# Moving most of an attention stage beside the first quarter of a selective scan, in a one-core fusion kernel on Trainium2

## The chip, the cores and the metric

The kernel runs on one NeuronCore of one Trainium2 chip. A core has a matrix engine (PE, TensorE; its weight loads are listed as PEld), a vector engine (DVE), a scalar engine (ACT), GpSimd (POOL), and SP, which here only issues transfers. The engines run their own instruction lists and meet at semaphores. The metric is the device time of the kernel in microseconds (us); lower is better.

## What is computed

Sixteen images of 3 x 128 x 128 become 64 patch tokens each (width 192), pass a 12-head attention, are joined with 32 text tokens each, and go through a selective scan and a quantized feed-forward layer, both added to the residual.

```python
t = conv(x, conv_w, stride 16) + conv_b              # 16 x 64 tokens x 192
q, k, v = (t @ w.T + b for w, b in ...)              # 12 heads of 16
out = softmax(q k^T / 4) v ; h = out @ wo.T + bo
h = concat([h, txt], axis=1)                         # 16 x 96 x 192
# selective scan on layernorm(h): D_IN = 384, N = 16 states
xi, res = split(layernorm(h) @ W_in); xc = silu(causal_conv4(xi))
delta = softplus(x_dbl[:48] @ W_dt + b_dt)           # x_dbl = xc @ W_x, also gives B and C
y = scan(xc, delta, A, B, C) + xc * D ; h = h + (y * silu(res)) @ W_out
h = h + ffn(layernorm(h))                            # two linear layers with quantized activations and weights
```

## The kernel before

**Quarters, blocks and steps.** The 16 images are four quarters of 4 images (4 x 96 = 384 tokens). The scan of a quarter is 24 steps: the 384 channels are 3 blocks of 128, and each block has 8 steps of two states each. Step g of the 96 is: ACT `decay` (L972, two exponentials of 128x384 into PSUM), POOL `times_b` (L457, the scan's input), DVE `scan` (L1278), ACT `guards` (L981, two), DVE `guard_states` (L1287, or L1284 on steps 1, 4 and 6 of a block), then the product with C, on POOL (`times_c`, L463) in five steps of eight and on DVE (L1293) in steps 1, 4 and 6, and PE `sum_y` (L787), which adds the product up in PSUM. ACT works one step ahead with `decay`, POOL two ahead with `times_b`.

**Everything else of the scan's stage and of the feed-forward layer lies beside the steps.** A table `AT` of step numbers says at which step each piece of work of each quarter is put. Every engine goes through the steps in order and issues there what is due, in the order of its own `beside`, `amid` or `after`; no engine looks ahead. Work that uses a PSUM bank is a job: `begin` on PE waits until the reader of the bank's last job has left it. Banks 0 to 4 belong to the scan, 5 to 7 to the jobs.

**The attention precedes the scan.** PE makes the tokens of all 16 images (the helper at L585, 24 products of 128x512, two instructions each), then queries, keys and values. A pair of images is one round: POOL `block_keys` (L416) multiplies the keys of a pair by a head mask into a block-diagonal `kbd`; PE `scores`; DVE takes the maxima and subtracts them (`softmax_in`, L1190 and L1193); ACT exponentials (L1089); PE `turn_prob` (L650), ACT copy (L1084); PE `values`; DVE `softmax_out` (L1200, L1203); PE `turn_out` (L673), ACT copy (L1099); PE `project`; DVE `add_bo` (L1209) writes the result into `h`. The eight pairs are pipelined in a loop written by hand. Quarter 0's mixer (norm, `xi` and `z` products, the causal convolution L1233, `silu_u` L1249, the products with W_x and W_dt, the softplus L952 to L962 and L1255 to L1270) is placed by hand into the last rounds, and quarter 1's norm and `xi` into the steps -6 to 2.

**Transfers.** SP issues all loads at the start in one list, then `rows(q)`: eight transfers of 768 KB which spread B and C of the quarter, stored by ACT (L945) to DRAM, over the 128 lanes of `bc`. Before the scan `bc` holds the images' patches, the attention's queries and keys, and the convolution's weights, so quarter 0's `rows` waits for the last `scores`.

```python
for g in range(STEPS):            # DVE
    scan(g)
    amid(g)
    guard_states(g)
    after(g)
    if on_vector(g):
        times_c(g)
```

## Time and profile before

| what | value |
|---|---|
| median of 3 runs (lowest, highest) | 589.78 us (589.7, 590.13) |
| the profiled execution: its own time | 589.52 us |
| its span, first to last instruction | 587.7 us |
| busy: PE, DVE, ACT, POOL | 404.6, 451.9, 359.1, 411.5 us |
| mean granted TensorE clock | 0.818 of full |
| moved by DMA | 34.35 MB |

A busy time is the union over the instructions of an engine. The granted clock is 1.0 at 2.4 GHz and 0.5 at 1.2 GHz. The profiled execution is 0.3 us from the median of the runs. The rows themselves stand in a section below.

### The profile page before, as it was taken

Reading aid. Unit: us, or ns where it says so; the run is one execution under the profiler, and the core shown is the slowest. Engines: PE = TensorE matmul, PEld = TensorE weight load, DVE = VectorE, ACT = ScalarE, POOL = GpSimd, SP = SyncE. Lnnn points to the kernel's source line nnn. Section 1 sums busy time; section 2 is a strip of 40 time slices with the busy share of each in tenths; the row PEclk is TensorE's granted clock in tenths of the full one; section 3 lists DMA queues with packets and bytes.
Section 4 is the critical chain, followed back from the end, with each engine's and each line's share of the span. In section 5 each row is a group of like instructions: output and inputs, shape, how many; then the busy total and the mean of one; then the engine's idle time right before and its main releaser. Section 6 shows DMA issues by size and latency. Waiting matters only on the chain.

```text
span 587.7 us, 5261 instructions
## 1 busy us (share of the span) xinstructions
PE 404.6 (69%) x1498; PEld 217.9 (37%) x1498; DVE 451.9 (77%) x531; ACT 359.1 (61%) x642; POOL 411.5 (70%) x332
## 2 busy tenths in 40 slices
PE   5998997852697493876665649676755956665553
PEld 2336754431333251543332316333322532332423
DVE  1234644349999999898899898999999799998341
ACT  1135342486689674668775756997657677962353
POOL 2035510094789985879997788799879999988442
PEclk9999998968777685785877988978767797987865
DMA  8900000280000044100004330000154100000000
GB/s 313 196 1 1 2 2 0 86 347 0 1 6 0 26 179 169 58 0 1 0 0 158 124 148 4 20 1 1 44 173 160 54 18 3 1 0 1 20 2 20
DMA packets 10269, 34.35 MB, mean 58 GB/s; under 512 B 2064, under 2 KB 4960, under 8 KB 10016
## 3 DMA queue, kind: packets, MB, share of 16 engines
q1 hardware_dynamic: 9840, 33.23, 16.6%
q10 hardware_dynamic: 400, 0.79, 0.4%
q8 instruction: 12, 0.20, 0.1%
q14 instruction: 17, 0.14, 0.1%
HBM read 32.64 MB, written 1.38 MB: 58 GB/s over the span
## 4 chain that ended last, share of the span: by engine, by line
POOL 36%; DVE 19%; issue 14%; ACT 5%; PE 4%; DVEq 0%; POOLq 0%; ACTq 0%
POOL big L457 15%; POOL big L463 11%; DVE PS L1278 8%; PE PS L585 3%; DVE big L1287 2%; DVE big L1293 2%; ACT PS L972 2%; ACT big L981 2%; POOL big L500 2%; POOL big L481 1%; DVE big L1233 1%; POOL big L475 1%; POOL big L435 1%; POOL big L439 1%; POOL big L490 1%
## 5 line engine op out<-in xcount | busy, mean ns | idle before, releaser
L787 PE MATMUL PS<-big,eighth 128*128 128x384 f32 x384 | 192.1, 640 | 115.5 <-POOL big L463 100.2
L457 POOL TENSOR_TENSOR big<-big,bc 128x768 f32<-128x768 f32 x96 | 179.8, 1882 | 0.0
L1278 DVE TENSOR_TENSOR_SCAN PS<-PS,big 128x768 f32<-128x768 f32 x96 | 168.3, 1753 | 6.4 <-ACT PS L972 4.6
L787 PEld LDWEIGHTS PS<-big,eighth 128*128 128x128 f32 x384 | 87.4, 242 | 201.5 <-POOL big L463 128.6
L972 ACT ACTIVATE PS<-big,Aneg 128x384 f32<-128x384 f32 x192 | 103.8, 573 | 92.7 <-DVE big L1293 56.5
L463 POOL TENSOR_TENSOR big<-big,bc 128x768 f32<-128x768 f32 x60 | 108.7, 1812 | 52.8 <-DVE big L1287 52.5
L981 ACT ACTIVATE big<-big,guard,Ahalf 128x380 f32<-128x380 f32 x192 | 122.2, 690 | 0.0
L1287 DVE SCALAR_TENSOR_TENSOR big<-big,PS 128x768 f32<-128x768 f32 x60 | 56.9, 949 | 5.6 <-DVE PS L1278 0.9
L416 POOL TENSOR_TENSOR big<-bc,cst_sb 96x1536 f32<-96x1536 f32 x8 | 22.0, 2754 | 44.4 <-ACT bc L879 33.3
L585 PE MATMUL PS<-big,w_in_sb 96*128 96x384 f32 x96 | 41.3, 568 | 5.0 <-DVE big L1233 4.4
L585 PE MATMUL PS<-big 128*64 128x34 f32 (+3 forms) x416 | 43.1, 281 | 0.0
L1284 DVE SCALAR_TENSOR_TENSOR PS<-big,PS 128x768 f32<-128x768 f32 x36 | 34.7, 963 | 3.8
L585 PEld LDWEIGHTS PS<-big 96*64 96x64 f32 (+2 forms) x416 | 30.1, 144 | 15.5 <-issue 14.0
L426 POOL TENSOR_SCALAR rstd<-bmv 96x4 f32<-96x4 f32 x4 | 2.8, 688 | 45.5 <-DVE bmv L1223 45.3
L1293 DVE TENSOR_TENSOR big<-PS,bc 128x768 f32<-128x768 f32 x36 | 34.1, 947 | 0.2
L585 PEld LDWEIGHTS PS<-big,w_in_sb 96*128 96x128 f32 x96 | 21.6, 231 | 22.2 <-issue 13.7
L585 PE MATMUL PS<-f_in_q,big 96*96 96x512 bf16 x64 | 23.7, 492 | 6.9 <-DVE big L1323 5.4
L585 PE MATMUL PS<-bc 128*96 128x512 f32 x48 | 23.3, 649 | 6.7 <-DMA bc<-in_cw_dram 6.7
L784 PE MATMUL PS<-big,diagD 128*128 128x384 f32 x24 | 16.5, 784 | 14.4 <-DVE big L1299 14.4
L500 POOL TENSOR_TENSOR big<-big,g_out_bc 96x512 f32<-96x512 f32 x16 | 20.1, 1262 | 7.8 <-ACT big L1017 7.8
L1190 DVE TENSOR_REDUCE big<-PS 128x12 f32<-128x768 f32 x8 | 7.6, 952 | 21.5 <-PE PS L585 21.5
L1023 ACT ACTIVATE big<-big,magic 96x512 f32<-96x512 f32 x16 | 11.9, 802 | 19.9 <-POOL big L519 19.0
(139 smaller groups left out, 560.6 us busy)
## 6 DMA issues: line engine op xcount, KB each, us to landing
bc<-bc_rows SPq DMA_DIRECT2D x32, 768.0 KB, 4.4
bc<-in_x_cols_dram SPq DMA_DIRECT2D x3, 512.0 KB, 6.7
bc<-in_x_cols_dram SPq DMA_DIRECT2D x1, 1536.0 KB, 10.0
out_dram<-h SPq DMA_DIRECT2D x4, 288.0 KB, 2.7
big<-in_f_in_dram SPq DMA_DIRECT2D x1, 768.0 KB, 12.4
bc<-in_cw_dram ACTq DMA_DIRECT2D x1, 576.0 KB, 5.9
w_in_sb<-in_w_in_dram SPq DMA_DIRECT2D x1, 576.0 KB, 16.9
big<-in_f_out_dram SPq DMA_DIRECT2D x1, 384.0 KB, 14.6
```

The lines of the kernel that those rows point to most:

```text
L416: P.tensor_tensor(kbd[:, p % 2], kT[:, hf, :, c:c + 128].unsqueeze(2).broadcast_to([F, 2, HPT, 128]), headmask.unsqueeze(1).unsqueeze(3).b ...
L457: P.tensor_tensor(pair(vR[:, g % VRING]), part(du, q, m).unsqueeze(1).broadcast_to([128, PAIR, QT]), rows_of(g, 0), ALU.mult).then_inc(sem ...
L463: P.tensor_tensor(v, v, rows_of(g, 1), ALU.mult).then_inc(sem("c_pool"), 1)
L500: P.tensor_tensor(yf[:, b], yf[:, b], g_out_bc[:, :], ALU.mult).then_inc(sem("yg_ready"), 1)
L585: return pe.matmul(o_, l_, r_, start=start, stop=stop)
L787: ins = pe.matmul(y_sum, eighth[:, :], vR[:, g % VRING, QT * e:QT * (e + 1)], start=False, stop=True, skip_group_check=True)
L972: ins = A.activation(state_of(g, e), part(delta, q, m), ACT.Exp, scale=Aneg[:, PAIR * j + e, m:m + 1])
L981: ins = A.activation(gR[:, g % GRING, QT * e:QT * (e + 1)].rearrange("p (b l) -> p b l", b=QB)[:, :, 0:L - 1], lt[:, :, 1:L], ACT.Tanh, bi ...
L1278: V.tensor_tensor_scan(h_, h_, vR[:, g % VRING], 0.0, ALU.mult, ALU.add).then_inc(sem("scan_done"), 1)
L1284: V.scalar_tensor_tensor(states(g), gR[:, g % GRING], 1.0, states(g), ALU.add, ALU.mult).then_inc(sem("guarded_here"), 1)
L1287: V.scalar_tensor_tensor(vR[:, g % VRING], gR[:, g % GRING], 1.0, states(g), ALU.add, ALU.mult).then_inc(sem("guarded"), 1)
L1293: V.tensor_tensor(pair(vR[:, g % VRING]), pair(states(g)), rows_of(g, 1), ALU.mult).then_inc(sem("c_vector"), 1)
```

## The change

Names of the new kernel are its own; its line numbers differ from those of the kernel before.

- **Patches by quarters.** The product that makes tokens is done quarter by quarter (`patch`, 256 columns instead of 512), and so are queries, keys and values (`project_tokens`, `values_of_tokens`). The weights `cw` come in three transfers instead of one.
- **Only quarter 0's attention (pairs 0 and 1) is ahead of the scan.** The scores of pair 2 and the patches of quarters 2 and 3 are placed at steps -13 to -10, while quarter 0's softplus runs; the patches' copies out of PSUM (`patch_out`) stand in ACT's list at steps 0 and 1. Pairs 3 to 7, and the rest of pair 2, are placed in steps 0 to 22. So are queries, keys and values of quarters 2 and 3, quarter 0's `z`, and quarter 1's norm, `turn` and `xi`, which preceded or opened the scan before.
- **Attention work becomes jobs** in the table `AT`, with the banks 5 to 7 from step -12 on; before that step all eight banks serve. The softmax goes by halves of six heads (128x384 instead of 128x768).
- **Key blocks by DMA.** POOL's `block_keys` is gone. `kbd` is set to zero once, and SP copies the keys of each head into its diagonal block: six transfers a quarter of 16 lanes.
- **SP's list.** Text tokens are loaded by quarters, each after the quarter's value product; `w_in` and what follows stand behind quarter 0's key blocks. `rows(0)` waits, from its sixth transfer on, for the last patch product of quarter 3, and key blocks of quarters 2 and 3 follow behind it.
- **Quarter 0's mixer** runs by blocks of 128 channels (`silu_u` and its tanh too); its norm is applied by DVE (`normed`) instead of ACT; the quantization of the feed-forward weights is split in two pieces that stand in DVE's list at steps -21 and -16.
- From step 24 on the table is unchanged.

```diff
-FIRST_MIXER = dict(stats=-6, root=-6, xn=-5, turn=-5, turned=-4, xi0=-3, xi1=-2, xi2=-2, tap0=0, tap1=0, tap2=1,
...
-FIRST_STEP, LAST_STEP = -6, STEPS + 32
...
+for p, steps in enumerate((
+        dict(sc0=-29, sc1=-29, si0=-29, si1=-28, ex0=-29, ex1=-28, tp0=-27, tp1=-26, pt0=-27, pt1=-26, vo=-25, so=-25,
...
+        dict(sc0=-13, sc1=-13, si0=-13, si1=-13, ex0=-11, ex1=-11, tp0=-10, tp1=-10, pt0=0, pt1=0, vo=1, so=1,
+             to=2, at=2, pj=3, ab=3),
...
+for p, first in ((4, 5), (5, 7), (6, 13), (7, 16)):
+    AT.update({(name, p): first + r for name, r in dict(
+        sc0=0, sc1=1, si0=0, si1=1, ex0=1, ex1=2, tp0=2, tp1=3, pt0=2, pt1=3, vo=4, so=4, to=5, at=5, pj=6, ab=6).items()})
+AT.update({("ws", 0): -26, ("wmean", 0): -24, ("f_in", 0): -21, ("f_out", 0): -16})
+FIRST_STEP, LAST_STEP, WIDE_BEFORE = -32, STEPS + 32, -12
...
     for i, key in enumerate(JOBS):
-        open_ = range(6, 8) if i < FRONT_JOBS else range(5, 8) if i < WIDE_FROM else range(8)
-        left = AT.get((LAST_READ["%s%d" % (key[0], key[2])], key[1]), FIRST_STEP - FRONT_JOBS + i)
+        open_ = range(8) if JOB_STEP[key] < WIDE_BEFORE or i >= WIDE_FROM else range(5, 8)
...
+            def key_blocks(q):
+                job_left(sp, "k", q, 0)
+                if q == 0:
+                    sp.wait_ge(sem("kbd_set"), 1)
+                else:
+                    job_here(sp, "sc", 2 * q - 1, 1)
+                for j in range(HPT):
+                    lanes = slice(HD * j, HD * (j + 1))
+                    sp.dma_start(kbd[lanes, :, j, :], kT[lanes, :, :]).then_inc(sem("ld_kbd"), 16)
...
+            def text(q):
+                job_here(sp, "v", q, 0)
+                load("txt", h[NP:L, QB * q:QB * (q + 1), :], txt[QB * q:QB * (q + 1)].rearrange("b l d -> l b d"))
...
-            load("ffn", f_out_raw, f_out.rearrange("p m n -> p (m n)"))
-            load("txt", h[NP:L, :, :], txt.rearrange("b l d -> l b d"))
+            key_blocks(0)
...
+            patches(1, 0, KT)
             load("mix", w_in_sb[:, :, :], w_in)
...
             load("mix", w_dt_sb[:, :], w_dt)
             load("mix", w_out_sb[:, :, :], w_out)
+            patches(2, 0, KT)
+            patches(3, 0, KT)
             load("g", g_in_bc[:, :], g_in.partition_broadcast(F))
             load("g", g_out_bc[:, :], g_out.partition_broadcast(F))
+            key_blocks(1)
+            text(1)
...
-                if q == 0:
-                    sp.wait_ge(sem("s_ps"), PAIRS)
...
+                    if q == 0 and j >= 3:
+                        job_here(sp, "patch", min(j - 3, 1) if j < 5 else NQ - 1, 1)
...
                 rows(q)
+                if q == 0:
+                    key_blocks(2)
+                    text(2)
+                    key_blocks(3)
+                    text(3)
...
-            def block_keys(p):
-                hf, c = p // 4, (p % 4) * 128
-                pool.wait_ge(sem("qkv_sb"), 8 if hf == 0 else 12)
-                if p >= 2:
-                    pool.wait_ge(sem("s_ps"), p - 1)
-                P.tensor_tensor(
-                    kbd[:, p % 2],
-                    kT[:, hf, :, c:c + 128].unsqueeze(2).broadcast_to([F, 2, HPT, 128]),
-                    headmask.unsqueeze(1).unsqueeze(3).broadcast_to([F, 2, HPT, 128]),
...
+                if due("plus0", g):
+                    for m in range(CT):
+                        pool.wait_ge(sem("tt_ready"), m + 1)
+                        series_a(0, m)
+                        pool.wait_ge(sem("half_series"), m + 1)
+                        series_b(0, m)
+                        if m == 0:
+                            times_u(0, 0)
+                            edges(0, 0)
...
+            def patch(q, m):
+                o_ = begin("patch", q, m)
+                for k in range(KT):
+                    if q == 0 and m == 0 and k % 2 == 0:
+                        pe.wait_ge(sem("ld_cw%d" % k), 16)
+                        pe.wait_ge(sem("ld_x0_%d" % k), 16)
+                    if q and m == 0 and k == 0:
+                        pe.wait_ge(sem("ld_x%d_0" % q), 16)
+                    ins = mm(o_[0:F, 0:QP], cw_sb[:, k, F * m:F * (m + 1)], xs[q][:, k, :], k == 0, k == KT - 1)
+                done(ins, "patch")
...
+            def scores(p, m):
+                if p % 2 == 0 and m == 0:
+                    pe.wait_ge(sem("ld_kbd"), 16 * LOADS["kbd"] * (p // 2 + 1))
+                    job_left(pe, "qy", p // 2, 0)
+                o_ = begin("sc", p, m)
+                for b2 in range(2):
+                    t = NP * (2 * (p % 2) + b2)
+                    ins = mm(o_[64 * b2:64 * b2 + 64, 0:HPT * NP], qT[:, m, t:t + NP], kbd[:, m, :, t:t + NP], True, True)
+                done(ins, "sc")
...
+            def prob_out(p, m):
+                job_here(act, "tp", p, m)
+                if p:
+                    job_here(act, "vo", p - 1, 0)
+                A.activation(pT[:, m].rearrange("p g q -> p (g q)"), job_bank("tp", p, m)[:, 0:3 * 128], ACT.Copy
+                             ).then_inc(sem("left_tp"), 1)
...
+            def softplus_in():
+                for m in range(CT):
+                    dt_out(0, m)
+                for m in range(CT):
+                    exps(0, m)
+                for m in range(CT):
+                    logs(0, m)
...
+                        exp_scores(p, m)
+                for p in due("at", g):
+                    out_turned(p)
+                for m in range(2):
+                    for p in due("pt%d" % m, g):
+                        prob_out(p, m)
+                for q in due("k_out", g):
+                    keys_out(q)
+                for q in due("q_out", g):
+                    queries_out(q)
+                for q in due("v_out", g):
...
+            def softmax_in(p, m):
+                sc = job_bank("sc", p, m)[:, 0:HPT * NP].rearrange("p (j t) -> p j t", j=HPT)
+                job_here(dve, "sc", p, m)
+                link(V.tensor_reduce(smax[:, m, :], sc, AX.X, ALU.max))
+                if p:
+                    job_here(dve, "tp", p - 1, m)
+                V.tensor_tensor(prob[:, m].rearrange("p (j t) -> p j t", j=HPT), sc,
+                                smax[:, m, :].unsqueeze(2).broadcast_to([128, HPT, NP]), ALU.subtract
+                                ).then_inc(sem("left_sc"), 1)
...
+            def normed():
+                dve.wait_ge(sem("norm_b"), 1)
+                for b in range(QB):
+                    ins = V.tensor_scalar(xn[:, b, :], h[:, b, :], bmv[:, b, 0:1], rstd[:, b:b + 1], ALU.subtract, ALU.mult)
+                ins.then_inc(sem("xn_ready"), 1)
```

**DVE at the scan's entry.** Before, from the scan over `later` of block 0 to step 1; `states` is `PS`, L1287 and L1284 are `guard_states`, L1233 is quarter 1's convolution:

```order
L1270 SCALAR_TENSOR_TENSOR big<-keep,big 128x384 [waits delta_ready]
L1278 SCALAR_TENSOR_TENSOR PS<-PS,big 128x768 [waits v_ready,a_ready]
L1287 SCALAR_TENSOR_TENSOR big<-big,PS 128x768 [waits scan_done,g_ready]
L1278 SCALAR_TENSOR_TENSOR PS<-PS,big 128x768 [waits v_ready,a_ready]
L1284 SCALAR_TENSOR_TENSOR PS<-big,PS 128x768 [waits scan_done,g_ready]
L1233 SCALAR_TENSOR_TENSOR big<-PS,v,big 128x4x95 [waits tap_ready,job_xi]
```

The same place in the changed kernel (L1330 is `scan`, L1235 and L1238 are `softmax_in` of pair 3, L1245 and L1248 `softmax_out` of pair 2):

```order
L1322 SCALAR_TENSOR_TENSOR big<-keep,big 128x384 [waits delta_ready]
L1330 SCALAR_TENSOR_TENSOR PS<-PS,big 128x768 [waits v_ready,a_ready]
L1339 SCALAR_TENSOR_TENSOR big<-big,PS 128x768 [waits scan_done,g_ready]
L1235 TENSOR_REDUCE big<-PS 128x6 [waits job_sc]
L1238 TENSOR_TENSOR big<-PS,big 128x384 [waits job_tp,dve_chain]
L1235 TENSOR_REDUCE big<-PS 128x6 [waits job_sc]
L1238 TENSOR_TENSOR big<-PS,big 128x384 [waits job_tp,dve_chain]
L1330 SCALAR_TENSOR_TENSOR PS<-PS,big 128x768 [waits v_ready,a_ready]
L1336 SCALAR_TENSOR_TENSOR PS<-big,PS 128x768 [waits scan_done,g_ready]
L1245 RECIPROCAL big<-PS 128x12 [waits job_vo]
L1248 TENSOR_TENSOR big<-PS,big 128x192 [waits job_to,dve_chain]
```

Between the first and the second scan DVE now waits for the scores of pair 3.

**PE just ahead of step 0, in the changed kernel** (L641 on `bc` are the patch products of quarters 2 and 3, L707 `turn_prob` of pair 2, L641 of 64x384 the scores of pair 3, L823 the first product of step 0's sum):

```order
L641 MATMUL PS<-bc 96x256 [waits left_x]
L641 MATMUL PS<-bc 96x256 x5
L707 MATMUL PS<-cst_sb,big 128x128 [waits left_dt,prob_ready]
L707 MATMUL PS<-cst_sb,big 128x128 x2
L707 MATMUL PS<-cst_sb,big 128x128 [waits left_patch,prob_ready]
L707 MATMUL PS<-cst_sb,big 128x128 x2
L641 MATMUL PS<-bc 96x256 [waits ld_x3_0,left_patch]
L641 MATMUL PS<-bc 96x256 x5
L641 MATMUL PS<-bc 96x256 [waits left_tp]
L641 MATMUL PS<-bc 96x256 x5
L641 MATMUL PS<-big 64x384 [waits left_tp]
L641 MATMUL PS<-big 64x384
```

The copies that set `left_patch` stand in ACT's list behind the work of steps 0 and 1; in the kernel before nothing of this stood there:

```order
L1033 ACTIVATE PS<-big,Aneg 128x384 [waits left_sc,left_v]
L1033 ACTIVATE PS<-big,Aneg 128x384
L1042 ACTIVATE big<-big,guard,Ahalf 128x4x95 [waits later_ready]
L1042 ACTIVATE big<-big,guard,Ahalf 128x4x95
L906 ACTIVATE h<-PS,v 96x256 [waits job_patch] x2
L949 ACTIVATE big<-PS 128x384 [waits job_vo,job_tp] x2
```

So part of the patch work of quarter 3 lies behind ACT's `decay` of step 1 and `guards` of step 0.

## Rows read from the trace of the kernel before

**Rows 1.** Busy time of each engine by stage, with the granted clock

```profile
core 0: us, PE busy (x) PEld busy (x) DVE busy (x) ACT busy (x) POOL busy (x), PEclk, DMA share, GB/s
47.00:95.00 48.00, 42.16 (x390) 29.04 (x385) 26.90 (x49) 22.46 (x43) 18.10 (x10) 1.00 0.00 1
...
129.71:182.66 52.95, 33.33 (x69) 14.58 (x68) 50.59 (x51) 40.37 (x68) 39.92 (x26) 0.76 0.01 5
182.66:233.78 51.12, 34.10 (x82) 17.30 (x80) 50.12 (x54) 33.28 (x61) 42.05 (x28) 0.73 0.28 103
129.71:233.78 104.07, 67.43 (x149) 31.88 (x147) 100.71 (x104) 73.65 (x128) 81.97 (x53) 0.75 0.14 53
...
233.78:587.70 353.92, 230.48 (x699) 125.04 (x698) 301.16 (x327) 235.55 (x425) 291.18 (x244) 0.79 0.12 43
```

**Rows 2.** DVE in order of time: scans of steps 0, 1, 13 and 24

```profile
129.71 1.77 DVE L1278 TENSOR_TENSOR_SCAN PS<-PS,big 128x768 f32<-128x768 f32 x1 [4.57 <-ACT PS L972]
...
132.82 1.76 DVE L1278 TENSOR_TENSOR_SCAN PS<-PS,big 128x768 f32<-128x768 f32 x1
...
182.66 1.76 DVE L1278 TENSOR_TENSOR_SCAN PS<-PS,big 128x768 f32<-128x768 f32 x1
...
233.78 1.76 DVE L1278 TENSOR_TENSOR_SCAN PS<-PS,big 128x768 f32<-128x768 f32 x1
```

**Rows 3.** Who waited for whom, 129.71 to 233.78 us: total, times, longest

```profile
PE PS L787 <- POOL big L463: 27.3, 9, 6.3
POOL big L463 <- DVE big L1287: 17.8, 6, 7.0
ACT PS L972 <- DVE big L1287: 14.5, 6, 4.3
```

**Rows 4.** PE in order of time, to 64 us

```profile
6.71 23.27 PE L585 MATMUL PS<-bc 128*96 128x512 f32 x48 [6.71 <-DMA bc<-in_cw_dram]
...
29.96 16.80 PE L585 MATMUL PS<-big 96*96 96x512 f32 x96
...
58.56 1.52 PE L585 MATMUL PS<-big,bc 96*64 96x384 f32 x8
...
63.77 1.52 PE L585 MATMUL PS<-big,bc 96*64 96x384 f32 x8
```

**Rows 5.** Groups by line and shape, 47 to 129.71 us: busy, mean ns

```profile
L585 PE MATMUL PS<-big 96*64 96x96 f32 x64 | 2.9, 246 | 0.0
...
L1209 DVE TENSOR_TENSOR h<-PS,bo_bc 64x384 f32<-64x384 f32 x8 | 4.4, 550 | 15.3 <-PE PS L585 15.3
...
L1203 DVE TENSOR_TENSOR big<-PS,big 128x192 f32<-128x192 f32 x8 | 2.9, 358 | 0.3
...
L1200 DVE RECIPROCAL big<-PS 128x12 f32<-128x12 f32 x8 | 1.8, 225 | 7.2 <-PE PS L585 7.2
...
L1243 DVE SCALAR_TENSOR_TENSOR big<-big,PS 128x384 f32<-128x384 f32 x3 | 1.5, 542 | 0.0
```

**Rows 6.** ACT in order of time: quarter 0's x_out to the table load

```profile
110.29 0.49 ACT L942 ACTIVATE big<-PS 96x384 f32<-96x384 f32 x1 [2.88 <-PE PS L585]
...
117.78 1.34 ACT L958 ACTIVATE big<-big 128x384 f32<-128x384 f32 x3
119.14 1.28 ACT L962 ACT_TABLE_LOAD   x1
```

**Rows 7.** POOL in order of time, ahead of the first scan

```profile
127.02 0.21 POOL L445 TENSOR_TENSOR big<-ones,edge 128x4 f32<-128x4 f32 x1
127.17 5.34 POOL L457 TENSOR_TENSOR big<-big,bc 128x768 f32<-128x768 f32 x3
```

**Rows 8.** DMA issues: KB each, median us from issue to landing

```profile
bc<-bc_rows SPq DMA_DIRECT2D x32, 768.0 KB, 4.4
...
w_in_sb<-in_w_in_dram SPq DMA_DIRECT2D x1, 576.0 KB, 16.9
...
bc_rows<-big ACTq DMA_DIRECT2D x8, 24.0 KB, 1.6
```

586 lines of the change are left out of this document (259 added, 327 removed), and 7 rows, old and new, of tables (PE_JOBS, series_a).

## The prediction

> **What bounds the kernel now.** I first read the busy times by stage. From 129.71 us, the scan of step 0, to 233.78 us, the scan of step 24, DVE is busy for 100.7 of 104.1 us; POOL has 82.0, ACT 73.7, PE 67.4 at a granted clock of 0.75 [rows 1, 2]. So a step of the first quarter takes 4.34 us and DVE, at 97%, sets it. The other engines' waits in that stretch agree: ACT's next `decay` and POOL's `times_c` wait for DVE's guard (14.5 and 17.8 us in total), and PE waits 27.3 us for POOL's product [rows 3]. Ahead of step 0 it is the reverse. From 47 to 95 us, the attention's rounds, PE is busy 42.2 of 48.0 us at full clock and DVE 26.9 [rows 1]; a round lasts from one pair's scores at 58.56 to the next's at 63.77 us, that is 5.2 us, all of it PE's [rows 4]. Nothing of the scan runs in these 129.7 us, a fifth of the kernel, in which DVE has little to do. The change moves attention from a stretch that PE sets into one that DVE sets.
>
> I cut the time at two marks, the scan of step 0 (the entry) and the scan of step 24. Before: 129.7 + 104.1 + 353.9 = 587.7 us, and 1.8 us lie outside the span (589.52 is the profiled execution's time; the median of the runs is 0.3 us above it).
>
> **The entry.** What must still precede it, with durations of the rows before:
> - Patches of quarter 0: a quarter of the 23.3 us [rows 4], 5.8 us, and up to 9 at the half clock with which PE begins (this first product took 23.3 us for 48 instructions, 0.48 us each on average, on 512 columns). The start itself was 6.71 us, the landing of the weights; now the first third of them and a smaller patch piece suffice, so I take 4 to 5 us. Tokens at about 12 us.
> - Keys: 16.8 us was for queries and keys of four quarters and values of two [rows 4]; less 2.9 for the values [rows 5], a quarter's keys are 1.7 us, and ACT's copies 0.8: 15 us.
> - Key blocks: no row of before shows a copy inside the core by DMA. The nearest are 24 KB in 1.6 us and 768 KB in 4.4 us [rows 8]; six issues one behind the other at 0.4 us, and a landing between these: 4 to 7 us, nearest to the small one. I take 4.5. Scores at 19.5 us. The Trainium skill, "DMA: Bandwidth & Descriptors", Anatomy of one DMA, gives a fixed cost of about 2.0 us for one transfer, measured on another queue; by it the estimate would be 0.4 us higher, and the row of 1.6 us speaks against it.
> - Two pairs: each goes through the full chain of scores, softmax, turn, values, turn, projection, some 12 us for one alone by its durations, and 3 us for the second behind it: 34.5 us. The 3.7 us of weight quantization now stand on DVE between the two `add_bo`, which costs 1.5: 36.5.
> - Norm, turn, `xi`, convolution, `silu_u`, W_x of quarter 0: DVE 1.5 + POOL 1.4 + DVE 1.0 (`normed` has no row; four operations of 96x192 lie between 0.2 and 0.53 us each) + PE and ACT 3 + three convolution blocks of 1.9 and their ends: 53.5 us for the W_x product's copy.
> - From that copy to the entry it was 110.29 to 129.71, 19.4 us [rows 6, 2]. In the change the three dt copies no longer wait for attention (about 2 us off), and the table load that stood before the first `decay` is behind an earlier exponential (1.3 off [rows 6]). But POOL now does the series of blocks 1 and 2 behind the edges instead of ahead of them, some 3 us, before its first `times_b` of 1.8 us [rows 7]: 16 to 19 us, taken 16.5.
>
> Entry at **70 us**, bounds 65 and 76. That is 59.7 us less than 129.7.
>
> **Steps 0 to 23.** What is added on DVE: ten half softmaxes at 1.1 us (two operations of 384 columns, 0.55 each as in L1209), six `softmax_out` (0.22 + 0.36), six `add_bo` (0.55) [rows 5], quarter 1's statistics 1.5, quarter 0's three `z` products at 0.54 [rows 5]: 11 + 3.5 + 3.3 + 1.5 + 1.6 = 20.9 us. Of it 13.7 fall in steps 0 to 12, which also lose quarter 1's `silu_u` (1.5), and 8.7 with that in 13 to 23. DVE then needs 62.8 and 58.9 us.
>
> On PE: five whole rounds of 5.2 us, the rest of pair 2 (3.1), queries, keys and values of two quarters (9.8), patches of quarter 3 (5.1), quarter 0's `z` (4.4), turn and `xi` of quarter 1 (5.3): 53.7 us at full clock. What PE had there, 67.4 us at 0.75, is 50.6 at full clock, so 104.3 together, 62.8 of it in steps 0 to 12 and 41.5 behind (W_x and dt of quarter 1 move across). In the first half PE needs as much as DVE. The highest busy share that the trace shows for PE with such jobs is 42.2 of 48.0, 0.88 [rows 1], since each job waits for copies of others; 62.8 / 0.88 = 71.4 us. I take this for steps 0 to 12, and for 13 to 23 DVE with its present share (50.12 of 51.12): 60.1 us. ACT gains about 24 us and reaches 98, which both bounds hide; POOL loses nothing but gains 1.4.
>
> At the entry there is a hole besides. DVE's second scan stands behind the softmax of pair 3, its scores behind quarter 3's patches on PE, these behind `patch_out` on ACT, and this behind `decay` 0 and 1 and `guards` 0. Scan 0 to scan 1 were 3.1 us [rows 2]. By the durations (decays 2.2, guards 1.3, copies 0.8, patches 5.1, scores 0.7) the scores are ready about 10 us after `decay` 0 begins, when DVE has been idle for 2.6 us; if PE runs at half clock there, 5 more. I add 3.0. `rows(0)` issues its last three transfers behind the same patches; they land 4.4 us later and more [rows 8], while POOL asks for the sixth in its eighth product: covered, unless PE is at half clock. Of the clock the rows show 1.00 while PE is busy 0.88 of the time, 0.75 where it is busy 0.65 [rows 1]. The Trainium skill, "TensorE: Matmul & The Clock Gate", Part 1, says that the slow state is the default and activity ends it; the rows agree, and by it a fuller PE would run these steps nearer to full clock, as I assume.
>
> Steps 0 to 23: 71.4 + 60.1 + 3.0 = **134.5 us**, 30.4 more than now.
>
> **From step 24 on** the tables are the same: 353.9 us. SP's key blocks and text stand between `rows(0)` and `rows(1)`; they end by step 13, and `rows(1)` is due at step 16.
>
> Sum: 70.0 + 134.5 + 353.9 + 1.8 = **560.2 us**, 29.3 less than the profiled execution.
>
> **Rivals.**
> - *DVE alone sets the steps.* PE fits in between and the hole closes: 62.8 at its present 0.955 is 65.8, plus 60.1, is 125.9. For it: POOL and PE have six ring places between them and DVE. Against: PE's 0.88. 70 + 125.9 + 355.7 = 551.6; with the entry at its lower bound 547. Chance 0.14.
> - *PE at the present clock.* If it stays at 0.75, steps 0 to 12 are 83.7 us of PE without a gap and 95 at its share of 0.88; with 60 to 62 behind, 70 + 144 to 157 + 355.7 = 570 to 583. For it: PE waits on many small jobs. Against: full clock from 47 to 95. Chance 0.16.
> - *The entry comes late.* SP's list is in order and `w_in` is issued only behind the key blocks, near 20 us; it landed 16.9 us after its issue in the crowd of before [rows 8] and is needed near 42. If it or the key blocks slip, the entry is at 76 to 80 us: 566 to 570. The change would then do only part of what it says. Chance 0.07.
> - *Lockstep, slower than before.* ACT's list is in order: `decay` of step g+1 stands behind copies that wait for PE jobs, which stand behind `sum_y`, which waits for POOL's product, which waits for DVE's guard of step g. Fully in series a step is scan 1.9, guard 0.9, product 1.8, sum 1.5, PE jobs 3.3, copy 0.8, `decay` 1.1: 11.3 us, and 13 such steps give 70 + 147 + 60.1 + 355.7 = 633. It decides from 24 steps in 163.8 us on (104.1 + 59.7), 8.0 us a step in the first 13 against my 5.7. Against: most jobs have a step or two between their parts in the table. Chance 0.05.
>
> **How the numbers follow.** My forecast has 0.58, with 552 to 569 as its own range (entry 65 to 76, hole 0 to 8). The range for 8 in 10 takes in the lower bound of the first rival and half of the second's: 547 to 577. About 0.2% (1.2 us) is what a measurement of this kernel can tell from no change. All cases but the last are faster: faster 0.94; within 0.2% 0.01; slower 0.05.
>
> **What would show it.** Right: the scan of step 0 near 70 us; scan 24 near 204; between them PE busy over 80% with a granted clock above 0.9, and DVE near 90%; a gap of DVE before pair 3's softmax of 2 to 8 us; from scan 24 to the end 354 us. Wrong: a gap before quarter 0's first scores that ends with the key blocks' landing and is over 5 us; scan 24 later than 220 us with PE's clock under 0.8; ACT waits on PE at each step; a different length behind step 24, which I count as unchanged.

## The result, and the profile after

The changed kernel takes **610.57 us** (median of 4 runs, 609.8 to 612.53) against 589.95 us before (4 runs, 589.7 to 596.79): a ratio of the means of 1.033 (95% interval 1.025 to 1.040). It is slower by about 20 us; forecast was 560.2, with 547 to 577 as the range. Medians and ratios in this document leave out the executions that were over 1.5% above the fastest of the same kernel (two of run 12's ten).

Busy times after, by the same stages as [rows 1] and with the same columns; the scans of steps 0, 13 and 24 are the marks:

```profile
core 0: us, PE busy (x) PEld busy (x) DVE busy (x) ACT busy (x) POOL busy (x), PEclk, DMA share, GB/s
...
20.00:44.00 24.00, 20.77 (x100) 13.11 (x101) 10.44 (x20) 5.29 (x12) 0.00 (x0) 0.50 0.56 162
...
80.58:169.29 88.71, 68.27 (x342) 40.65 (x340) 61.80 (x83) 45.71 (x94) 44.63 (x31) 0.88 0.10 33
169.29:252.86 83.57, 53.28 (x226) 28.34 (x226) 55.45 (x70) 46.57 (x85) 38.56 (x27) 0.81 0.19 68
80.58:252.86 172.28, 121.55 (x568) 68.99 (x566) 117.25 (x152) 92.28 (x178) 83.19 (x58) 0.85 0.15 50
252.86:609.30 356.44, 233.27 (x698) 127.34 (x698) 300.85 (x326) 237.18 (x427) 290.63 (x244) 0.78 0.12 42
```

| stretch | before | forecast | after |
|---|---|---|---|
| to the scan of step 0 | 129.7 | 70.0 | 80.6 |
| steps 0 to 12 | 53.0 | 74.4 | 88.7 |
| steps 13 to 23 | 51.1 | 60.1 | 83.6 |
| from step 24 | 353.9 | 353.9 | 356.4 |

So 49.1 us are won ahead of the scan, and 68.2 are lost in the 24 steps. Read the 172.28 row against [rows 1]: before, DVE was busy for 97% of the stretch and was its bound. Now it has 117.3 of 172.3 us, 68%, and PE has 71%. **No engine's own work is the bound any more.** What takes the time are waits (who waited for whom in this stretch; total, times, longest):

```profile
POOL big L522 <- DVE big L1339: 69.5, 12, 15.3
...
DVE big L1339 <- ACT big L1042: 16.0, 7, 4.4
ACT big L989 <- PE PS L641: 15.3, 4, 10.4
DVE big L1235 <- PE PS L641: 14.5, 6, 5.2
ACT big L949 <- PE PS L707: 13.9, 6, 9.2
```

In the same steps of the kernel before, DVE's guard waited for ACT once, for 0.5 us, and the three others did not occur. DVE's guard (L1339) waits for ACT's `guards`; ACT's copies (L949 of the turned probabilities, L989 of `z`) wait for PE; DVE's softmax (L1235) waits for PE's scores. They form a ring, and at scans 9 and 10 it can be followed. DVE, PE and ACT in order of time, three answers:

```profile
134.23 1.75 DVE L1330 TENSOR_TENSOR_SCAN PS<-PS,big 128x768 f32<-128x768 f32 x1
136.09 0.96 DVE L1336 SCALAR_TENSOR_TENSOR PS<-big,PS 128x768 f32<-128x768 f32 x1
136.96 0.55 DVE L1351 TENSOR_TENSOR big<-PS,big 128x384 f32<-128x384 f32 x1
145.19 1.90 DVE L1285 SCALAR_TENSOR_TENSOR big<-PS,v,big 128x380 f32<-128x380 f32 x3 [7.67 <-ACT big L982]
...
148.40 1.75 DVE L1330 TENSOR_TENSOR_SCAN PS<-PS,big 128x768 f32<-128x768 f32 x1
153.07 0.95 DVE L1339 SCALAR_TENSOR_TENSOR big<-big,PS 128x768 f32<-128x768 f32 x1 [2.92 <-ACT big L1042]
```

```profile
137.57 1.65 PE L823 MATMUL PS<-big,diagD 128*128 128x384 f32 x2 [3.14 <-DVE big L1351]
139.01 2.77 PE L826 MATMUL PS<-big,eighth 128*128 128x384 f32 x4
141.70 1.80 PE L641 MATMUL PS<-big 128*64 128x34 f32 x24
143.44 0.55 PE L707 MATMUL PS<-cst_sb,big 128*128 128x128 f32 x3
147.23 5.46 PE L641 MATMUL PS<-big,w_in_sb 96*128 96x384 f32 x8 [3.25 <-DVE big L1285]
```

```profile
144.02 0.49 ACT L949 ACTIVATE big<-PS 128x384 f32<-128x384 f32 x1 [9.15 <-PE PS L707]
144.41 0.67 ACT L982 ACTIVATE big<-PS,v 128x384 f32<-128x384 f32 x1
150.17 0.67 ACT L982 ACTIVATE big<-PS,v 128x384 f32<-128x384 f32 x1 [5.10 <-PE PS L641]
150.74 1.08 ACT L1033 ACTIVATE PS<-big,Aneg 128x384 f32<-128x384 f32 x2
151.75 1.29 ACT L1042 ACTIVATE big<-big,guard,Ahalf 128x380 f32<-128x380 f32 x2
```

Step 8 begins a new block, so PE's first y product (L823) needs the gate (L1351, the product with which DVE takes the finished block out of the sum's bank). DVE has it only in step 9: PE stands for 3.14 us, until 137.57. Pair 4's values and pair 5's turn (L707) stand behind it in PE's list; ACT's copy waits 9.15 us for them; quarter 1's first tap (L982, with which ACT starts the convolution from the `xi` product) stands behind the copy; DVE's convolution (L1285) waits 7.67 for the tap. Then the ring closes through the banks: PE's next `xi` products (147.23) need the bank that the convolution leaves, ACT's second tap waits for them, and `decay` and `guards` stand behind that tap, so DVE waits again, at 153.07. Scan 10 starts 14.2 us after scan 9; it was 4.1 before the change.

The lists are not all of this gap: PE works for 6.4 us between the gate and the end of the turn at a mean granted clock of 0.60, and the eight `xi` products at 147.23 take 5.46 us at 0.50, where eight of the same shape took 2.82 us near full clock (at 51.98). By these numbers an estimated 5 us of the 14.2 are the clock's.

### The profile page after: what moved, and what is told of

The parts are those of the page before. It is cut to its first block, busy times and chain, and to the rows that moved or that the text cites. A ratio compares the mean times of both kernels' runs of the same rounds, so it can differ in the third digit from the quotient of the medians.

```text
span 609.3 us, 5539 instructions
## 1 busy us (share of the span) xinstructions
PE 419.5 (69%) x1578; PEld 238.2 (39%) x1578; DVE 450.4 (74%) x553; ACT 361.3 (59%) x668; POOL 387.4 (64%) x323
## 4 chain that ended last, share of the span: by engine, by line
POOL 34%; DVE 17%; issue 14%; PE 14%; ACT 7%; DVEq 0%; POOLq 0%; ACTq 0%
POOL big L516 14%; POOL big L522 10%; PE PS L641 8%; DVE PS L1330 6%; PE PS L826 4%; ACT big L1042 2%; DVE big L1339 2%; ACT PS L1033 2%; DVE big L1345 2%; DVE big L1285 2%; POOL big L559 1%; POOL big L540 1%; POOL big L534 1%; POOL big L494 1%; POOL big L549 1%
## 5 line engine op out<-in xcount | busy, mean ns | idle before, releaser
L826 PE MATMUL PS<-big,eighth 128*128 128x384 f32 x384 | 186.1, 622 | 105.7 <-POOL big L522 86.6
L1330 DVE TENSOR_TENSOR_SCAN PS<-PS,big 128x768 f32<-128x768 f32 x96 | 168.2, 1752 | 8.4 <-POOL big L516 7.7
L1339 DVE SCALAR_TENSOR_TENSOR big<-big,PS 128x768 f32<-128x768 f32 x60 | 57.0, 949 | 20.1 <-ACT big L1042 16.0
L641 PE MATMUL PS<-big 128*64 128x34 f32 (+2 forms) x320 | 45.0, 358 | 6.0 <-DMA big<-big 3.0
L641 PE MATMUL PS<-big,w_in_sb 96*128 96x384 f32 x96 | 43.8, 594 | 5.1 <-DVE big L1285 3.2
L641 PEld LDWEIGHTS PS<-big 128*64 128x64 f32 (+1 forms) x320 | 26.9, 164 | 22.0 <-issue 12.1
L1285 DVE SCALAR_TENSOR_TENSOR big<-PS,v,big 128x380 f32<-128x380 f32 (+2 forms) x36 | 21.8, 607 | 14.3 <-ACT big L982 13.4
L641 PE MATMUL PS<-bc 128*96 128x256 f32 x96 | 28.9, 472 | 4.8 <-DMA bc<-in_x_cols_dram 4.8
L823 PE MATMUL PS<-big,diagD 128*128 128x384 f32 x24 | 16.9, 803 | 20.5 <-DVE big L1351 20.5
L641 PEld LDWEIGHTS PS<-big,w_in_sb 96*128 96x128 f32 x96 | 21.5, 235 | 23.4 <-issue 17.2
L641 PE MATMUL PS<-f_in_q,big 96*96 96x512 bf16 x64 | 24.4, 505 | 6.9 <-DVE big L1375 5.4
L1235 DVE TENSOR_REDUCE big<-PS 128x6 f32<-128x384 f32 x16 | 8.9, 555 | 22.7 <-PE PS L641 22.3
L641 PEld LDWEIGHTS PS<-bc 128*96 128x96 f32 x96 | 19.8, 211 | 14.1 <-DMA bc<-in_cw_dram 4.8
```

Of the source, the lines that this page charges most:

```text
L641: return pe.matmul(o_, l_, r_, start=start, stop=stop)
L826: ins = pe.matmul(y_sum, eighth[:, :], vR[:, g % VRING, QT * e:QT * (e + 1)], start=False, stop=True, skip_group_check=True)
L1285: ins = V.scalar_tensor_tensor(xv[:, :, s:L], xi[:, :, 0:L - s], convw[:, j, KW - 1 - s:KW - s], xv[:, :, s:L], ALU.mult, ALU.add)
L1330: V.tensor_tensor_scan(h_, h_, vR[:, g % VRING], 0.0, ALU.mult, ALU.add).then_inc(sem("scan_done"), 1)
L1339: V.scalar_tensor_tensor(vR[:, g % VRING], gR[:, g % GRING], 1.0, states(g), ALU.add, ALU.mult).then_inc(sem("guarded"), 1)
```

## The experiments

The theory is that of the **lists**: every engine takes its list in order, so one late job delays what stands behind it on three engines. Rivals are the **clock** (PE at half speed after gaps) and sheer **load**. "Steps" below is the time from scan 0 to scan 24. Runs 1 to 10 and 13 to 15 were executed once each. The kernels of runs 11, 16 and 12, each with 6 to 8 executions, spread over 3.2, 4.1 and 8.1 us, so a difference of under 4 us between single executions carries nothing by itself; more weight lies on the waits that the traces show gone or new.

**1. The gate a step earlier.**

```diff
+AT.update({("yg0", 0): 8, ("yg1", 0): 16, ("yg2", 0): 24})
```


> The three gates of quarter 0 stand one step earlier in the table (after scans 8, 16 and 24 instead of 9, 17 and 25). Theory of the lists (TensorE's first product of a new block waits for a gate that VectorE has a step too late, and the attention jobs behind it make ScalarE and then VectorE late): the stalls behind scans 9 and 17 shrink, steps 0 to 23 take 172.3 less 8 to 20 us, span 589 to 601. Theory of the clock (TensorE at half speed after idle gaps is what costs): 0 to 3 us less. Theory of sheer load (VectorE and TensorE simply have more to do): no change, 609 within 1.

Measured: 600.87 us, span 599.1, steps 163.6 (8.6 less). Scan 9 to 10 fell from 14.2 to 8.3 us, 17 to 18 from 15.1 to 8.0. These two stretches are 13.0 us shorter; others grew by 4.4 in return (13 to 14 from 5.5 to 8.3). It is the smaller end of what the lists say, and over twice what I gave clock or load. But from scan 9 to 10 PE now had the full clock, so part of the 5.9 us there is the clock's. Over all the steps it is not: its mean was 0.84 for 0.85.

**2. Other jobs ahead of the y products.**

```diff
-    beside(g)
+    if g < 1 or g > QSTEPS:
+        beside(g)
+    if 0 <= g < QSTEPS:
+        beside(g + 1)
     if 0 <= g < STEPS:
         sum_y(g)
```


> TensorE issues the other work of step g+1 ahead of the y products of step g, for steps 0 to 23. Theory of the lists: no attention product waits any more behind a y product that waits for a gate or for GpSimd, so ScalarE's copies and VectorE's work come in time; steps 0 to 23 take 10 to 25 us less than 172.3, span 584 to 599. Theory of the clock: 0 to 5 us less, since the same idle gaps only change place. Theory of load: no change, 609 within 1. If the loops close through the three shared banks and not through the order of the list, it gains under 5 us as well.

Measured: 594.39 us, span 592.6, steps 160.3 (12.0 less), scan 0 at 78.2. ACT's 9.15 us wait of before is now:

```profile
134.95 0.49 ACT L952 ACTIVATE big<-PS 128x384 f32<-128x384 f32 x1 [2.85 <-PE PS L707]
...
140.08 0.67 ACT L985 ACTIVATE big<-PS,v 128x384 f32<-128x384 f32 x1 [4.07 <-PE PS L641]
```

The same work in another order, at the same mean clock of 0.85 in the steps: neither load nor, over all the steps, the clock is the cause of these 12 us. The second row is the ring through the banks, and that stays: PE's `xi` products still wait 3.25 us there for the convolution.

**3. The same at the two block changes alone** (steps 8 and 16).

```diff
-    beside(g)
+    if g not in (BLOCK + 1, 2 * BLOCK + 1):
+        beside(g)
+    if g in (BLOCK, 2 * BLOCK):
+        beside(g + 1)
     if 0 <= g < STEPS:
         sum_y(g)
```

> On the changed kernel, TensorE's other work of the next step goes ahead of the y products in two steps alone, 8 and 16 (the first y product of a block follows there and waits for VectorE's gate); in the other 22 steps the order stays. If the wait for the gate at the block changes is what the changed order removed (the run with all 24 steps: 172.3 to 160.3 us), this one keeps 9 to 12 us of it: steps 0 to 23 take 160 to 163 us, span 597 to 600. If the y products held up the attention jobs in every step (they wait for GpSimd's product there), it keeps 3 us or less: 169 to 172 us. Theory of load: 172.

Measured: 604.39 us, span 602.5, steps 165.5: 6.8 us of the 12.0. Between the two expectations. Scans 9 to 10 and 17 to 18 are 13.1 us shorter (6.4 and 9.8 us), and 6.3 us of this come back in other stretches, which run 2 avoids in part. That over half of the 12 is the gate at the block changes rests on single executions.

**4. Filler ahead of the first scores.**

```diff
+    if g == -29:
+        pe.wait_ge(sem("alog_ready"), 1)
+        for _ in range(8):
+            mm(bank(7)[:, 0:QT], ones[:, :], keep[:, :], True, True)
```


> Eight products of ones by the keep row (128x384) into a bank that is free then are added on TensorE ahead of the first scores, where it waited 2.99 us for the key blocks' DMAs; nothing reads them. Theory of the clock: the granted clock stays at 1.00 between 20 and 43 us where it was 0.50, TensorE's work of that stretch (about 17 us busy) halves, scan 0 comes 4 to 9 us before 80.6 and the span falls as much, to 600 to 605. If the front's length is that of its chain over three engines, scan 0 moves by under 2 us. Steps 0 to 23 keep their 172 us in either case.

Measured: 605.41 us, span 603.6; scan 0 at 75.61, steps 171.6. In the changed kernel PE waits 2.99 us for the key blocks (PE in order of time, the first row below) and then has the half clock for 20 us and more (two stretches of the changed kernel, the next rows). The last row is the run with the filler, 20 to 44 us, at 0.93:

```profile
21.33 3.47 PE L641 MATMUL PS<-big 96*64 96x384 f32 x10 [2.99 <-DMA big<-big]
```

```profile
28.00:36.00 8.00, 7.52 (x45) 6.07 (x44) 1.79 (x7) 2.61 (x6) 0.00 (x0) 0.50 0.84 251
36.00:44.00 8.00, 6.57 (x38) 4.69 (x37) 5.10 (x7) 0.62 (x2) 0.00 (x0) 0.50 0.00 0
```

```profile
20.00:44.00 24.00, 20.83 (x130) 13.43 (x129) 11.94 (x29) 5.54 (x13) 1.22 (x2) 0.93 0.58 162
```

The clock theory holds for the front: scan 0 comes 5.0 us sooner, although the filler took 5.43 us on PE and the scores began 2.9 us later for it. Part of the 5.0 is variation: with the same lists ahead of it, scan 0 stood at 78.2 to 80.6 (the changed kernel, runs 1, 2, 3 and 7), and with the filler at 75.2 and 75.6 (runs 6 and 4), which is 4.1 us in the mean. Of the clock in the steps this run tells nothing; they kept their length.

**5. Less work on DVE.** For pairs 2 to 7 this kernel leaves out the maxima and differences of 60 of the 64 tokens of a head, so its output is not the attention's. The slice stands in all four operands of the two operations (one line is shown):

```diff
+    n = NP if p < 2 else 4
-    link(V.tensor_reduce(smax[:, m, :], sc, AX.X, ALU.max))
+    link(V.tensor_reduce(smax[:, m, :], sc[:, :, 0:n], AX.X, ALU.max))
```

> Leaves out most of the softmax's input side for pairs 2 to 7: maxima and differences are taken over 4 of the 64 tokens of each head (24 columns for 384), so about 10 us of VectorE's work beside the scan is gone and all waits stay. Theory of sheer load on VectorE: steps 0 to 23 take 8 to 10 us less than 172.3. Theory of the lists and of the clock: 0 to 4 us less, since VectorE is busy for only 117 of the 172 us.

Measured: 602.73 us, span 600.5, steps 165.1 (7.2 less). DVE's busy time in the steps fell by 7.4 us, to 109.9. This was my theory's miss: I expected 0 to 4, because DVE is idle a third of the time, and load's 8 to 10 comes nearer. I read it so: the softmax is a link of the ring (scores, softmax, exponential, turn), and a shorter link shortens the ring by nearly its full length. The stretches that shrank (scans 9 to 10 by 2.5 us, 7 to 8, 16 to 17 and 0 to 1 by 1.4 to 1.5 each) fit this, but a single execution does not show it. Idle time on DVE did not mean here that its work was free.

**6. The three edits together.**

> The edits of the first three runs in one kernel: gates a step earlier, TensorE's other work of step g+1 ahead of the y products of step g, eight filler products ahead of the first scores. If the early gate and the changed order remove the same stall (theory of the lists), their gains of 8.6 and 12.0 us in steps 0 to 23 do not add: 156 to 160 us for these steps, scan 0 near 73, span 583 to 588. If they removed different stalls they add: 151 to 152 us, span 579. Theory of the clock: no more than the filler's 5 us on top of 592.6.

Measured: 596.70 us, span 594.9, steps 164.1: 3.8 us *more* than with the jobs ahead alone, and outside all that I expected. The total says little in single executions; the new wait in the trace says more. With the jobs of step 8 now ahead of the y product of step 7, the early gate waits for that product. DVE and PE in order of time:

```profile
130.60 0.56 DVE L1359 TENSOR_TENSOR big<-PS,big 128x384 f32<-128x384 f32 x1 [4.13 <-PE PS L827]
```

```profile
127.72 1.56 PE L642 MATMUL PS<-big,w_in_sb 96*128 96x384 f32 x4
129.11 1.46 PE L827 MATMUL PS<-big,eighth 128*128 128x384 f32 x4
```

Each edit removes the wait between gate and product; both together turn it round, from PE for DVE to DVE for PE.

**7. The z products a step earlier**, on run 2.

```diff
+AT.update({("z1", 1): 15, ("tz1", 1): 15, ("zs1", 1): 16, ("z2", 1): 16, ("tz2", 1): 16, ("zs2", 1): 17})
```


> On top of the run with the jobs ahead (160.3 us for steps 0 to 23, span 592.6): the z products 1 and 2 of quarter 1 and what ScalarE and VectorE do with them come one step earlier (steps 15 and 16 instead of 16 and 17). There ScalarE waited 6.7 us for the last z product, with two table loads and the decay behind it, and VectorE then 4.0 and 2.3 us. Theory of the lists: the stretch from scan 18 to scan 19 (10.8 us) loses 4 to 7 us, and the span as much. Theory of load or of the clock: under 2 us. If the three shared banks only hand the wait on to the neighbours, under 2 us as well, and the stretch before scan 18 grows.

Measured: 590.37 us, span 588.6, steps 154.4 (5.9 less). Scan 18 to 19 fell from 10.8 to 3.8 us, as the lists say; but 16 to 17 grew by 4.2 (7.9 to 12.1), as the banks say. Scans 19 to 20 gave 3.4 more.

**8. Quarter 3's patches behind pair 3's scores**, on run 2.

```diff
-    job_here(sp, "patch", min(j - 3, 1) if j < 5 else NQ - 1, 1)
+    job_here(sp, "patch", min(j - 3, NQ - 1), 1)
...
+AT.update({("patch0", 3): 0, ("patch1", 3): 0})
```


> On top of the run with the jobs ahead (scan 0 at 78.2, scan 1 at 88.5, span 592.6): the patches of quarter 3 are multiplied behind the scores of pair 3, in step 0, and the rows' DMAs of block 5 wait for quarter 2's patches only. Theory of the lists: VectorE's wait of 4.3 us for the scores behind these patches goes, scan 1 comes 4 to 6 us sooner after scan 0, and 3 to 6 us of it are left at scan 24 (the 7 us of patches now stand ahead of the values of pair 2). Theory of load: TensorE's 7 us are only moved, 0 to 1 us.

This is the hole at the entry. PE and DVE of the changed kernel in order of time:

```profile
79.52 0.87 PE L707 MATMUL PS<-cst_sb,big 128*128 128x128 f32 x3 [3.80 <-ACT h L906]
80.19 7.56 PE L641 MATMUL PS<-bc 128*96 128x256 f32 x24
87.68 0.87 PE L641 MATMUL PS<-big 96*64 96x384 f32 x4
```

```profile
88.59 0.56 DVE L1235 TENSOR_REDUCE big<-PS 128x6 f32<-128x384 f32 x1 [5.18 <-PE PS L641]
```

Measured: 591.91 us, span 590.1. Scan 1 comes 4.9 us after scan 0 (10.3 in run 2), but at scan 24 only 1.9 us of the 5.5 are left, under my 3 to 6 and within what executions vary by: scans 1 to 2 grew by 3.4, as the patches delay pair 2's values instead.

**9. Pairs 2 and 3 ahead of the scan**, a partial undo; the steps of pair 2 (3) in the table, written together:

```diff
-sc=-13 (0), ex=-11 (1), tp=-10 (2), pt=0 (2), vo=1 (3), to=2 (4), pj=3 (5)
+sc=-13 (-9), ex=-11 (-8), tp=-10 (-7), pt=-10 (-7), vo=-9 (-6), to=-8 (-5), pj=-7 (-4)
-patch_out of quarter 2 (3) = 0 (1)
+patch_out of quarter 2 (3) = -10 (-9)
```

> Partial undo of the change on the changed kernel itself: the attention of pairs 2 and 3 (quarter 1) is finished ahead of scan 0, the patches of quarters 2 and 3 are copied out there too; only pairs 4 to 7 stay beside the steps. Scan 0 comes 6 to 14 us later than 80.6. Theory of the lists: most of the loss sits at the block changes in steps 9 and 17, which stay, so steps 0 to 23 lose only the hole at scan 1 and some 6 us of steps 2 to 8: 158 to 164 us, span 605 to 611. Theory of load (each pair beside the steps costs the same 68/6 = 11 us): 172.3 less 23 = 149 us, span 595 to 600.

Measured: 619.90 us, span 618.0; scan 0 at 97.0 (16.4 later, over my bound), steps 166.9 (5.4 less). This refutes load as the rule: two pairs taken out of the steps free 5.4 us and not 23. My own 158 to 164 is missed as well; the clock in the steps was lower here, 0.78 for 0.85. It also shows what two pairs cost alone: DVE, in order of time, stands between the links of a single pair.

```profile
88.65 0.55 DVE L1256 TENSOR_TENSOR h<-PS,bo_bc 64x384 f32<-64x384 f32 x1 [3.97 <-PE PS L642]
91.88 0.23 DVE L1246 RECIPROCAL big<-PS 128x12 f32<-128x12 f32 x1 [2.67 <-PE PS L642]
92.14 0.36 DVE L1249 TENSOR_TENSOR big<-PS,big 128x192 f32<-128x192 f32 x1
96.54 0.55 DVE L1256 TENSOR_TENSOR h<-PS,bo_bc 64x384 f32<-64x384 f32 x1 [4.05 <-PE PS L642]
97.02 1.75 DVE L1331 TENSOR_TENSOR_SCAN PS<-PS,big 128x768 f32<-128x768 f32 x1
```

Beside the steps these two pairs are cheap; the idea of the change is right for them.

**10. Quarter 1's patches and tokens later in the front** (again the steps in the table).

```diff
-patch=-21, patch_out=-21 and -20, k=-18, k_out=-17, qy=v=-17, q_out=v_out=-16; scores and softmax of pair 2 =-13
+patch=-18, patch_out=-13, k=k_out=qy=v=q_out=v_out=-13; scores and softmax of pair 2 =-12
```

> On the changed kernel, the patches of quarter 1 are multiplied behind quarter 0's turn and its first two conv products instead of ahead of them, and quarter 1's keys, queries and values behind dt. Where the front is held by TensorE's list (the patches took 7.2 us at half clock right ahead of the turn), scan 0 comes 4 to 7 us sooner than 80.6; if its chain over VectorE, ScalarE and GpSimd bounds it, 0 to 2 us. The scores of pair 2 come later then, so scan 1 may come up to 4 us later after scan 0, and scan 24 is sooner by 2 to 6 us. Theory of the clock: the patches' place doesn't matter, only their 3.6 us at half speed do, and the gain is under 3.6 us.

Measured: 633.63 us, span 631.8; scan 0 at 95.6, 15 us *later*. I had looked at PE alone. The keys come later, SP's `key_blocks(1)` waits for them, and `rows(0)`, which the scan's input needs, stands behind it on SP. SP and POOL in order of time:

```profile
84.84 3.88 SPq L395 DMA_DIRECT2D big<-big  x6
88.77 0.58 SPq L381 DMA_DIRECT2D h<-in_txt_dram  x1
89.39 15.29 SPq L443 DMA_DIRECT2D bc<-bc_rows  x8
```

```profile
93.72 1.82 POOL L517 TENSOR_TENSOR big<-big,bc 128x768 f32<-128x768 f32 x1 [8.11 <-DMA bc<-bc_rows]
```

In the changed kernel `rows(0)` was issued at 66.7. The steps took 182.0 us, 9.7 more; this was not followed up. So what this run tells of TensorE's list in the front is nothing; it tells of SP's.

**11. The combination** of runs 2, 4, 7 and 8.

> Jobs ahead of the y products, the z products of quarter 1 a step earlier, quarter 3's patches behind pair 3's scores, and the filler; the gates stay where the change put them. Theory of the lists: each removed a different stall, so they add: scan 0 near 75, steps 0 to 23 152 to 154 us, span 580 to 583, time 582 to 585, below the kernel before (589.5). If they share a stall: span 584 to 588. Theory of load: no sum, span near 590.

Measured: 585.82 us (8 runs, 584.3 to 587.6) beside 591.41 for the kernel before, ratio 0.991 (0.989 to 0.993). The profiled one is the fastest of the eight: scan 0 at 75.3, steps 151.2, span 582.5. The gains add (160.3 less 5.9 and 1.9 is 152.5).

**12. Third tap and quarter 3's keys later**, on run 11.

```diff
+("tap2", 1): 11, ("k", 3): 11, ("k_out", 3): 12
```


> On top of the combination: ScalarE's third tap of quarter 1 a step later (11, where VectorE needs it), and the keys of quarter 3 a step later on TensorE (11) and two on ScalarE (12). In steps 9 to 12 ScalarE waited for TensorE's tp, conv and key products with decay and guards of the next scans behind the wait (4.1, 2.9 and 1.2 us in the run with the jobs ahead), and VectorE then 1.9, 4.4 us. Theory of the lists: the stretch from scan 9 to scan 13 (27.7 us there, 13.4 before the change) loses 3 to 7 us and the span 3 to 6. If the shared banks hand the wait on (the keys' bank waits for the same conv), under 1.5 us. Theory of load: 0.

Measured: 590.4 us (8 runs, 583.0 to 591.1), ratio 0.996 (0.993 to 1.000); steps 158.5. Scans 9 to 13 lost 1.7 us only, and 13 to 14 grew from 5.3 to 11.7. A miss: the wait was handed on.

**13 to 15. Pairs a step later, and a shorter filler**, on run 11 (written here as the table's own lines).

```diff
-for p, first in ((4, 5), (5, 7), (6, 13), (7, 16)):
+for p, first in ((4, 5), (5, 8), (6, 13), (7, 16)):   # 13
+for p, first in ((4, 5), (5, 7), (6, 14), (7, 17)):   # 14
-        for _ in range(8):
+        for _ in range(4):                            # 15
```

> On top of the combination (584.3 to 587.6 us, scans 9 to 13 28.8 us apart where it was 13.4 before the change): pair 5's attention one step later (8 to 14 instead of 7 to 13), so that its scores, turned probabilities and values stand elsewhere between the conv products of quarter 1, all on three shared banks. Theory that the place of a pair between quarter 1's products makes the waits (banks and lists): the spacing from scan 9 to scan 15 changes by over 3 us in either direction, with the same work; the table as such is then worth several us per place. Theory of load: scan 24 within 1.5 us of the combination's 151.2 us after scan 0.

> On top of the combination: pairs 6 and 7 one step later (14 to 20 and 17 to 23 instead of 13 to 19 and 16 to 22). Theory of banks and lists: the spacing from scan 14 to scan 24 (67.6 us in the combination, 47.3 before the change) changes by over 3 us in either direction. Theory of load: within 1.5 us.

> The combination with four filler products instead of eight: eight took 5.43 us where TensorE was idle for 2.99, four take about 2.7. If idle time of TensorE ahead of the scores is what lets its clock fall, four keep it at 1.00 and scan 0 comes 2 to 2.7 us sooner than 75.3, span near 580. If they are too few, the granted clock is 0.50 behind 21 us again and scan 0 comes 3 to 5 us later, near 79.

Pair 5 later: 577.37 us, steps 146.7; scans 9 to 15 37.3 us apart for 43.6. With the same work, one step for one pair is worth 6 us there. Pairs 6 and 7 later: 583.39 us, steps 152.2; scans 14 to 24 67.3 us apart for 67.6. That is what load says, and my theory's "over 3 us" is missed. The places do move the waits (scans 14 to 17 are 7.5 us shorter), but all of it is given back by scan 24. Four filler products: 587.06 us, scan 0 at 75.0, only 0.3 sooner: the clock was 1.00 to 32 us but 0.67 from 32 to 40, where it was 0.84 in run 11. Neither of my cases came true, and eight products did no better than four here. Its steps took 3.9 us more; in a single run I can't tell that from variation.

**16 and 17. Timed.**

> The combination with pair 5 a step later, timed in rounds beside the kernel before. The look gave a span of 575.6 and 577.4 us, steps 0 to 23 146.7. If the place of the pair is the cause, it repeats: 576 to 580 us, ratio to the kernel before 0.975 to 0.983. If the look was one of the varying runs of such a table, the median lies at 582 to 586, ratio near 0.99.

> Pair 5 and pairs 6 and 7 one step later, on the combination. Pairs 6 and 7 alone moved scan 24 by 1.0 us (the stretch from scan 14 to scan 17 7.5 us shorter, given back by scan 24). Theory of banks and lists: gains of places do not add; anything from 574 to 583 us. Theory of load: the same as with pair 5 alone within 1.5 us.

Run 16: **581.17 us** (6 runs, 577.3 to 581.4), ratio 0.982 (0.979 to 0.984): the gain repeats, at 581 rather than 577, and is 4.6 us in the medians against run 11. Run 17: 580.11 us (4 runs, 579.4 to 581.6), ratio 0.983 (0.980 to 0.985), the same, which both cases allow. Either beats the kernel before (591.12 us beside them) by 10 us or more, and the changed one by 29. Run 16 by stages, in its fastest execution (the scan of step 24 is at 221.83, so the steps are 146.8 us and the rest 353.6):

```profile
0.00:75.00 75.00, 62.43 (x330) 39.49 (x332) 31.99 (x76) 31.93 (x65) 13.60 (x23) 0.93 0.54 162
75.00:221.50 146.50, 115.46 (x568) 67.34 (x564) 116.90 (x152) 91.25 (x176) 83.02 (x57) 0.88 0.16 56
221.50:575.50 354.00, 228.15 (x698) 124.61 (x698) 301.23 (x327) 237.19 (x428) 290.89 (x244) 0.80 0.12 42
```

DVE's work in the steps is the same 117 us as in the changed kernel, in 146.8 us instead of 172.3.

## Why the prediction was wrong

**The entry: 80.6 for 70.** Up to the scores the steps were good: tokens at 12.6 (12), key blocks issued from 16.0 (keys at 15), scores at 21.3 (19.5), DVE's `add_bo` of pair 1 at 43.6 (36.5), W_x copy at 64.2 (53.5), and 16.4 us from there (16.5). So the 10.6 us are 1.8 up to the scores, 5.3 in the two pairs and 3.6 in the mixer behind them, with 0.1 won at the end. What failed is "two pairs: ... some 12 us for one alone by its durations": those durations are of a PE at full clock, and here it had half, behind a gap that the key blocks' DMA itself made. The filler puts 4 to 5 of the 10.6 us on that. Another part is quarter 1's patches, which the sum had at nothing ahead of the turn; they took 7.2 us there (43.4 to 50.6) at a mean clock of 0.74. How much of it moving them alone would save stays open, since run 10 moved the keys too. The "half clock with which PE begins" is not in the rows either: the granted clock of the kernel before reads 1.00 up to 30 us, though the product instructions were slower at first (0.59 us each to 15 us, 0.39 after).

**Steps 0 to 23: 172.3 for 134.5.** The demands were right: DVE 117.3 us (121.7 forecast), PE 121.6 at a mean clock of 0.85, about 103 at full clock (104.3). What failed is how they were put together, "I take this for steps 0 to 12, and for 13 to 23 DVE with its present share". A share of busy time is a property of one order of the lists. The 0.88 came from a stretch that had only attention, DVE's 98% from the old order of the lists. In the new table a tap stands in the step of its product, and a copy in that of its turn; with three banks for the jobs, hand-overs between engines lie on the path (the 9.15, 7.67, 5.10 and 2.92 us in the rows above). With the same work, orders of the table took from 172.3 down to 146.7 us. In the first half run 13 meets my 74.4 us (73.8); it is in the second half, which I had called DVE's, that the best order still takes 72.9 us for 60.1.

**The hole at the entry: 8.1 us for 3.0.** The chain was named right (scores behind patches behind `patch_out` behind `decay`). The mis-sized term is the patches': 7.56 us for 5.1, with the first 4 us of them at half clock, so 2.5 of the "5 more" that I left out of the sum. With it DVE's idle time is the 5.18 us of the row for my 2.6. The rest of the 8.1 is work and one more wait that I had not put there: pair 3's two half softmaxes (2.2 us) and 0.97 us for the second half's scores.

**From step 24: 356.4 for 353.9.** Nearly as said; it was 353.6 in run 16.

**The rivals.** *Lockstep* is nearest to what happened, at 0.05. I had it as a full series in the first 13 steps, 11.3 us each; the real ring is looser there (6.8 us a step) and runs through the second half as well (7.6 us a step, which I had at 5.5). Its condition, 24 steps in over 163.8 us, was met. My argument against it, "most jobs have a step or two between their parts in the table", was wrong at just the places that count: gate and first y product, tap and `xi`, `z` and its copy. *PE at the present clock* came true in the front, where I had not looked for it. In the steps the mean clock was 0.85, and no run holds it at full, so its share of the loss stays open; between scans 9 and 10 it is an estimated 5 us. The gains of runs 1, 2 and 7 (8.6, 12.0 and 17.9 us) are not its doing: the mean was 0.84, 0.85 and 0.84 in them. *Late entry* came true at 80.6, but not through SP.

What stays open: the difference between 146.8 (in the fastest execution of run 16; its median is 4 us slower) and 134.5 us, and why executions of one kernel spread over 8 us in run 12. The banks' part is argued from the waits, since no run changed their number. Putting the values and the turned outputs into the unused columns of the states' banks, to have more than three banks, wasn't tried: ACT's `decay` writes those banks at the same time. The Trainium skill, "PSUM — Partial Sum Buffer", PSUM bank collisions raise a hardware error, says that a write by TensorE and one by ScalarE to the same bank and quadrant at once raise an error, disjoint columns included. No run here shows it.

## What to carry to other kernels

Before work is moved beside a tuned loop, write for each hand-over between engines what stands behind it in the waiting engine's list, and whether its operand is ready a step earlier. If not, count the chain's length, not the engines' demands: a share of busy time from another stretch is no forecast. Then try the table itself: moving one pair by one step, with the same work, was worth 6 us over six steps here (4.6 in the medians of the whole kernel), while moving two others (run 14) was worth nothing at scan 24, and three edits that looked sensible (runs 9, 10 and 12) made it slower. Follow the DMA queue's list too: it cost 15 us in run 10.
